# Neighbourhood attention: the layer-norm variance computed in a scores bank, one step later

## The chip, the cores and the metric

The kernel runs on one core of a Trainium2 chip. The metric is the device time of one execution in microseconds; lower is better. Everything is float32 unless a row says bf16.

## The reference, cut to what matters

A tower of token features, neighbourhood attention, a mixture of experts, a decayed attention and soft experts runs over 32 sequences of 512 tokens with 64 features. Between them stand layer norms without weights. The part that the change touches is the attention and the norm behind it:

```
h = h + _L0_attn_ref(_layernorm(h, axis=-1), ...)   # 31 neighbours, dilation 2, 8 heads of 8
h = h + _L0_ffn_ref(_layernorm(h, axis=-1), ...)    # this second norm is prepared inside the attention

def _layernorm(x, axis=-1, eps=1e-05):
    m = jnp.mean(x, axis=axis, keepdims=True)
    v = jnp.var(x, axis=axis, keepdims=True)
    return (x - m) / jnp.sqrt(v + eps)
```

The mean is taken out elsewhere (the features are kept in a basis where it is zero), so a norm is: squares of `h`, their mean over the 64 features (the variance), the logarithm and an exponential (together 1/sqrt), and a product.

## The kernel before, in words

The 32 sequences are 16 pairs (NP = 16); a pair's `h` is one 128 x 512 tile, the two sequences on two halves of the partitions. The attention with dilation 2 splits into even and odd tokens, so `neighbourhood_attention` (from L881) works on 32 units: unit u is pair u // 2 with even (u % 2 = 0) or odd tokens.

Each engine's program is written out by `unrolled` (L577): for step n = -6 ... 31 it calls a list of stages, each with a lead, on unit n + lead. The order of a list is the order in which that engine does the work. On TensorE (PE) a step is: scores of unit n+4 (`scores`, L1040: a mask by 16 bf16 matmuls, L1050, then 32 matmuls, L1056); in an even step the values of n+4 (`window_values`, L1001, matmul L1016), in an odd one the queries of a pair (L991); transposes of half 1 of the exponentials of n+3 (L1065); attention values of half 0 (L1079); keys of a pair (L984, even steps) or odd values (L1016, odd steps); attention values of half 1; transposes of half 0 of unit n+4; in even steps the projection of a pair (`project`, L1038), in odd steps the transposition of a pair's output (`turn`, L1028). Last, in steps 7, 15, 23 and 31, comes `spreads` (L1084): the variance of the quad of pairs that was finished last, four matmuls (L494) that put the means of the squares `s.sq` into 4 x 32 partitions.

PSUM has these tiles here: `p_s`, two tiles of two banks each, the scores of half 0 and half 1; `p_t`, two banks for the transposes; `p_o` for the attention values; and `p_m`, one bank that queries, keys, window values, the turned output, the projection and, before the change, the variance share one after another. Who may write `p_m` next is settled by waits: the variance waits for `s_otd` (ScalarE has copied the turned output out of `p_m`, L1154), and the next even values wait for `s.n_rstd` (ScalarE is done with the variance).

VectorE (DVE) takes for each half of the scores a maximum (L1176) and a difference (L1179, signal `s_diff`, one for each half of each unit), normalises (L1186, L1189), and adds the projection to `h` (L1198, signal `s_h`). ScalarE (ACT) takes the exponentials (L1139), copies transposes (L1146), values (L1133), keys (L1116), queries (L1109) and the turned output (L1154) out of PSUM, and for the norm does `deviations` (L1156): the logarithm (L1161, signal `s.n_ln`) and the exponential (L1163, signal `s.n_rstd`) of the variance. GpSimd (POOL) spreads the keys by head (L917), squares `h` (L487, signal `s.n_sq`) and scales it (L522) when a quad's 1/sqrt has come back. SP sends that result out (`hop`, L500) and back, broadcast over partitions (`spread`, L512), in `n_bc`.

Of the kernel before, what the change touches and what calls it, by code (L numbers as in the profile page):

```python
# [27 lines left out]
ACT = mybir.ActivationFunctionType  # L28
# [3 lines left out]
NP = NB // 2  # L32
NQ = NB // 4
LAST = NP // 4 - 1
# [438 lines left out]
def nth(stage, pair):  # L473

    return NP * stage + pair + 1


def quad(stage, n):

    return NP // 4 * stage + n + 1  # L480
# [47 lines left out]
def done(n):  # L528

    return n + (1 + CREDITS)  # L530
# [350 lines left out]
def neighbourhood_attention(nc, s, v):  # L881

    with ExitStack() as ctx:
# [3 lines left out]
        def ps(name, shape, n=1):  # L887
            return [ctx.enter_context(nc.psum_tensor(f"na_{name}{k}", shape, F32)) for k in range(n)]
# [4 lines left out]
        TURNS = 2 * NP  # L893
# [6 lines left out]
        on = [s.z[:, NP + 8 + k, :].rearrange("p (a b c d) -> p a b c d", a=2, b=2, c=2) for k in range(2)]  # L900
        ot = [s.z[:, NP + 10 + k, :].rearrange("p (two t) -> p two t", two=2) for k in range(2)]
        p_s = ps("ps", [128, 2, HL, 2, WIN], 2)
        p_t, p_o, p_m = ps("pt", [128, GROUPS // 2, 128])[0], ps("po", [128, 512])[0], ps("pm", [128, 512])[0]
        s_q, s_qd, s_k, s_kd, s_blk, s_v, s_vd, s_score, s_max, s_diff, s_e, s_et, s_etd, s_o, s_rden, s_on, s_ot, s_otd, s_out, s_h, s_derived = [
            sem(x) for x in ("q", "qd", "k", "kd", "blk", "v", "vd", "score", "max", "diff", "e", "et", "etd", "o", "rden", "on", "ot", "otd", "out", "h", "derived")]
# [69 lines left out]
        def _(te):  # L975
# [25 lines left out]
            def window_values(at):  # L1001
                j, par = at.of(2), at.k
                te.wait_ge(s_vd, done(at.n - 1))
                if par == 0:
                    te.wait_ge(s_qd, done(j))
                    te.wait_ge(s_otd, done(j - 2))
                    if j >= 6:
                        te.wait_ge(s.n_rstd, quad(1, (j - 6) // 4))
                else:
                    te.wait_ge(s_qd, done(min(j + 1, NP - 1)))  # L1010
                    te.wait_ge(s_h, done(j - 2))
# [28 lines left out]
            def scores(at):  # L1040
                j, par = at.of(2), at.k
                te.wait_ge(s_diff, done(2 * at.n - 1))
                if par == 0:
                    te.wait_ge(s_qd, done(j))
                    te.wait_ge(s_blk, done(j))
# [6 lines left out]
                for half, c, b, f in tiles:  # L1052
                    r = slice(32 * (2 * b + f), 32 * (2 * b + f) + 32)
                    t = 4 * half + c
                    w = window_start(t)
# [13 lines left out]
            def values(b):  # L1069
# [11 lines left out]
                    mm.then_inc(s_o, 1)  # L1081
                return stage

            def spreads(at):  # L1084
                if at.n % 8 == 7:
                    n = at.n // 8
                    te.wait_ge(s.n_sq, nth(1, 4 * n + 3))
                    te.wait_ge(s_otd, done(min(4 * n + 4, NP - 1)))
                    variance(nc, s, n, p_m).then_inc(s.n_var, 1)

            unrolled(TURNS, 2, (4, scores), (4, even_values), (6, queries),
                     (3, transposes(1)), (3, values(0)), (6, keys), (4, odd_values),
                     (3, values(1)), (4, transposes(0)), (1, project), (2, turn), (0, spreads))

        @block.scalar
        def _(sc):
# [52 lines left out]
            def fetch_output(at):  # L1149
                if at.k == 1:  # L1150
# [2 lines left out]
                    sc.wait_ge(s_out, done(j - 2))  # L1153
                    nc.scalar.activation(ot[j % 2].rearrange("p a b -> p (a b)"), p_m[:], ACT.Copy).then_inc(s_otd, 1)  # L1154

            def deviations(at):  # L1156
                if at.n % 8 == 7:
                    n = at.n // 8
                    sc.wait_ge(s.n_var, quad(1, n))
                    sc.wait_ge(s.n_z, nth(0, NP - 1))  # L1160
                    nc.scalar.activation(s.rstd[:, n, :], p_m[:], ACT.Ln, bias=s.eps[:]).then_inc(s.n_ln, 1)  # L1161
                    sc.wait_ge(s.n_ln, 2 + n)
                    nc.scalar.activation(s.rstd[:, n, :], s.rstd[:, n, :], ACT.Exp, scale=-0.5).then_inc(s.n_rstd, 1)  # L1163

            unrolled(TURNS, 2, (4, fetch_even_values), (6, fetch_queries), (3, fetch(1)), (4, exponential(0)),
                     (6, fetch_keys), (4, fetch_odd_values), (4, exponential(1)), (4, fetch(0)), (2, fetch_output), (0, deviations))

        @block.vector
        def _(ve):
# [995 lines left out]
```

## Time and profile before

| | us |
|---|---|
| median of 3 runs | 899.4 |
| lowest, highest | 893.36, 900.43 |
| profiled execution, its own time | 896.55 |
| its span in the trace | 894.8 |
| PE busy | 795.4 (89% of the span) |
| DVE, ACT, POOL busy | 576.0, 476.6, 304.9 |

The attention stage is the stretch from about 98 us to 387 us of the span. PE is the busiest engine there. "PEclk" is the granted clock of TensorE as a share of its full 2.4 GHz; 0.50 is the lower level, 1.2 GHz. In the rows, PEld is the weight load, which overlaps the matmuls, and "idle before" is what the engine stood still ahead of the row, with what ended it.

### The profile page before, as it was taken

To read this page: it belongs to the slowest core of one execution; us is meant where nothing else is said; L and a number is where in the kernel's file an instruction comes from. 1 tells how busy PE (TensorE), PEld (TensorE's weight loads), DVE (VectorE), ACT (ScalarE), POOL (GpSimd) and SP (SyncE) were. 2 spreads that over 40 slices of the span, in tenths; PEclk is the share of its full clock that TensorE was granted. 3 is DMA by queue.
4 is the path that set the end of the run, shared out by engine and by line. 5 is a ranking of instruction groups with operands and counts; after the bars stand their busy time and mean duration, and the time that the engine had idled before them with its cause. 6 is when DMAs were issued, how large, how long until landed. Compare 5 with 4: busy or idle time off the path is not lost. (4 is left out here: it accounts for less than half of the span.)

```text
span 894.8 us, 28767 instructions
## 1 busy us (share of the span) xinstructions
PE 795.4 (89%) x12566; PEld 405.7 (45%) x12566; DVE 576.0 (64%) x849; ACT 476.6 (53%) x656; POOL 304.9 (34%) x296
## 2 busy tenths in 40 slices
PE   4899499999998999758999989799996799999996
PEld 2222177676776766613333223376663233333332
DVE  5537176775775776545877865567673377777776
ACT  2244277776776777536566756422221355555553
POOL 4125553443463352121433455464453620000000
PEclk9889699999999999969999999999998699999998
DMA  4210401001001002010000130053331011111111
GB/s 109 22 28 1 130 28 51 5 4 62 4 4 62 4 5 62 3 60 1 1 2 1 51 92 1 13 167 91 89 94 36 8 30 48 48 49 49 48 49 36
DMA packets 38990, 36.83 MB, mean 41 GB/s; under 512 B 20881, under 2 KB 25138, under 8 KB 38738
## 3 DMA queue, kind: packets, MB, share of 16 engines
q1 hardware_dynamic: 37794, 33.04, 13.2%
q8 instruction: 100, 1.64, 0.8%
q10 hardware_dynamic: 1072, 1.95, 0.7%
q14 instruction: 24, 0.20, 0.1%
HBM read 19.24 MB, written 7.34 MB: 30 GB/s over the span
## 5 line engine op out<-in xcount | busy, mean ns | idle before, releaser
L2043 ACT ACTIVATE se_a<-se_p,cols 128x512 f32<-128x512 f32 x128 | 92.7, 774 | 76.9 <-PE se_p L1996 76.9
L1176 DVE TENSOR_REDUCE na_rowmax<-na_ps 128x16 f32<-128x1024 f32 x64 | 78.0, 1218 | 77.3 <-PE na_ps L1056 77.3
L2063 DVE SCALAR_TENSOR_TENSOR se_a<-se_p,cols,z 128x1024 f32<-128x1024 f32 x64 | 82.2, 1284 | 49.8 <-PE se_p L2006 49.8
L917 POOL TENSOR_TENSOR z<-na_k,const 128x512 f32<-128x512 f32 x64 | 64.6, 1042 | 139.9 <-ACT na_k L1116 139.9
L1418 ACT ACTIVATE z<-me_p,cols 128x512 f32<-128x512 f32 x128 | 81.1, 685 | 55.3 <-PE me_p L1357 50.5
L1550 DVE TENSOR_TENSOR me_gw<-me_pc,z 128x1024 f32<-128x1024 f32 x64 | 78.2, 1222 | 45.2 <-PE me_pc L1369 36.8
L487 POOL TENSOR_TENSOR n_sq<-h 128x512 f32<-128x512 f32 x64 | 68.4, 1074 | 96.2 <-DVE h L839 43.0
L1385 PE MATMUL me_py<-me_gw,w_out 64*64 64x512 f32 x512 | 88.1, 595 | 0.5 <-DVE me_gw L1550 0.5
L1357 PE MATMUL me_p<-z,moe_w 64*64 64x512 f32 x512 | 81.9, 614 | 5.7 <-ACT z L1418 5.7
L522 POOL TENSOR_TENSOR z<-h,n_bc 128x512 f32<-128x512 f32 x60 | 76.3, 1284 | 20.7 <-DMA n_bc<-n_spread 20.7
L1179 DVE TENSOR_TENSOR z<-na_ps,na_rowmax 128x1024 f32<-128x1024 f32 x64 | 78.3, 1224 | 2.2
L1996 PE MATMUL se_p<-z,f_w 64*64 64x512 f32 x512 | 70.5, 618 | 2.7 <-ACTq L535 1.8
L1065 PE MATMUL na_pt<-const,z 128*128 128x128 f32 x512 | 69.9, 280 | 2.6 <-ACT na_et L1146 1.7
L1146 ACT ACTIVATE na_et<-na_pt 128x1024 f32<-128x1024 f32 x64 | 65.4, 1022 | 7.7 <-PE na_pt L1065 6.9
L2006 PE MATMUL se_p<-se_a,f_w 64*64 64x512 f32 x512 | 68.7, 602 | 0.6 <-DVE se_a L2063 0.6
L1139 ACT ACTIVATE z<-z 128x1024 f32<-128x1024 f32 x64 | 67.4, 1053 | 1.7 <-DVE z L1179 0.8
L2018 PE MATMUL se_py<-se_a,w_out 64*64 64x512 f32 x512 | 67.4, 589 | 0.5 <-DVE se_a L2063 0.5
L1065 PEld LDWEIGHTS na_pt<-const,z 128*128 128x128 f32 x512 | 56.7, 142 | 15.6 <-issue 13.3
L1133 ACT ACTIVATE na_v<-na_pm 64x512 f32<-64x512 f32 x64 | 38.6, 602 | 30.2 <-PE na_pm L1016 29.8
L1282 POOL TENSOR_TENSOR h<-h,me_even 128x512 f32<-128x512 f32 x15 | 20.1, 1340 | 99.1 <-DVE me_even L1565 99.1
L1056 PE MATMUL na_ps<-z,na_q 32*32 32x256 f32 x2048 | 52.9, 401 | 0.1
L1079 PEld LDWEIGHTS na_po<-na_v,na_et 128*32 128x32 f32 x4096 | 41.7, 111 | 20.4 <-ACT na_et L1146 11.6
(300 smaller groups left out, 1266.0 us busy)
## 6 DMA issues: line engine op xcount, KB each, us to landing
n_bc<-n_spread SPq DMA_DIRECT2D x120, 128.0 KB, 3.0
z<-z SPq DMA_DIRECT2D x64, 128.0 KB, 2.4
out<-se_rows SPq DMA_DIRECT2D x16, 256.0 KB, 2.1
n_spread<-n_rstd SPq DMA_DIRECT2D x12, 256.0 KB, 2.0
const<-in_const ACTq DMA_DIRECT2D x1, 1050.0 KB, 6.9
const<-in_const ACTq DMA_DIRECT2D x1, 562.0 KB, 4.2
f_w<-in_L_ffn_W SPq DMA_DIRECT2D x4, 128.0 KB
const<-in_const ACTq DMA_DIRECT2D x1, 258.0 KB, 3.0
```

What stands on the lines that cost most here:

```text
L522: return eng.tensor_tensor(row(s.z, p), row(s.h, p), s.bc[p % 4][:], ALU.mult)
L1065: mm = nc.tensor.transpose(p_t[:, c, :], e[b][:, 2 * c:2 * c + 2, :].rearrange("p h w -> p (h w)"), const(s, "ident"))
L1176: nc.vector.tensor_reduce(rowmax[b][:], scored, AX, ALU.max).then_inc(s_max, 1)
L1179: nc.vector.tensor_tensor(e[b], scored, rowmax[b][:].unsqueeze(2).broadcast_to([128, GROUPS, WIN]), ALU.subtract).then_inc(s_diff, 1)
L1357: mm = nc.tensor.matmul(hidden(at.n, b)[half[e2], :], s.moe_w1[half[b], 2 * ep + e2, :], row(s.z, at.of(4))[half[b], :], start=True, stop= ...
L1385: mm = nc.tensor.matmul(p_y[half[b], e2, :], s.moe_w2[half[e2], ep, :], gw[at.k % 2][half[e2], b, :], start=(ep == 0 and b != e2), stop=(e ...
L1418: nc.scalar.activation(g[at.n % 7][:, b, :], hidden(at.n, b)[:], ACT.Gelu, bias=col(s, "moe_b1", ep)).then_inc(s_g, 1)
L1550: nc.vector.tensor_tensor(gw[at.k % 2][:], p_c[:], g[at.n % 7], ALU.mult).then_inc(s_gw, 1)
L1996: mm = nc.tensor.matmul(hidden(at.n, e2)[half[b], :], s.f1_w1[half[e2], 2 * ep + e2, :], z[half[e2], :], start=True, stop=True, skip_group ...
L2006: mm = nc.tensor.matmul(p_2[half[e2], b, :], s.f1_w2[half[b], 2 * ep + e2, :], a1[at.k % 2][half[b], e2, :], start=True, stop=True, skip_g ...
L2043: nc.scalar.activation(a1[at.k % 2][:, e2, :], hidden(at.n, e2)[:], ACT.Relu, scale=col(s, "f1_g1", 2 * ep + e2), bias=col(s, "f1_be1", 2 ...
L2063: nc.vector.scalar_tensor_tensor(out=a2[at.k % 2][:], in0=p_2[:], scalar=col(s, "f1_be2", ep), in1=s.f1_w[:, ep, :].unsqueeze(1).broadcast ...
```

## The change

The variance of quad n is computed one step later (steps 8, 16, 24 instead of 7, 15, 23), in another bank, and at another place within the step: between the attention values of half 1 and the transposes of half 0. The bank is the first of the scores tile of half 0, `p_s[0][:, 0]`. PE waits before it for the squares and for the difference of half 0 of the unit whose scores stand in the bank (unit 8n + 12), and the next unit's scores wait for the logarithm (`s.n_ln`). The even values no longer wait for `s.n_rstd`, the variance no longer waits for `s_otd`. On ACT, logarithm and exponential move with it: from the end of the step to between the exponential of half 1 and the copy of the transposes of half 0. The last quad's variance keeps its place at the very end, behind the loop, in the new bank.

```diff
+        p_var = p_s[0][:, 0].rearrange("p h a w -> p (h a w)")
...
                     te.wait_ge(s_otd, done(j - 2))
-                    if j >= 6:
-                        te.wait_ge(s.n_rstd, quad(1, (j - 6) // 4))
...
                 te.wait_ge(s_diff, done(2 * at.n - 1))
+                if at.n % 8 == 5 and at.n > 8:
+                    te.wait_ge(s.n_ln, 1 + at.n // 8)
...
+            def variance_of(n):
+                te.wait_ge(s.n_sq, nth(1, 4 * n + 3))
+                te.wait_ge(s_diff, done(2 * min(8 * n + 12, TURNS - 1)))
+                variance(nc, s, n, p_var).then_inc(s.n_var, 1)
+
             def spreads(at):
-                if at.n % 8 == 7:
-                    n = at.n // 8
-                    te.wait_ge(s.n_sq, nth(1, 4 * n + 3))
-                    te.wait_ge(s_otd, done(min(4 * n + 4, NP - 1)))
-                    variance(nc, s, n, p_m).then_inc(s.n_var, 1)
+                if at.n % 8 == 0 and at.n > 0:
+                    variance_of(at.n // 8 - 1)
...
-                     (3, values(1)), (4, transposes(0)), (1, project), (2, turn), (0, spreads))
+                     (3, values(1)), (0, spreads), (4, transposes(0)), (1, project), (2, turn))
+            variance_of(LAST)
...
+            def deviations_of(n):
+                sc.wait_ge(s.n_var, quad(1, n))
+                sc.wait_ge(s.n_z, nth(0, NP - 1))
+                nc.scalar.activation(s.rstd[:, n, :], p_var, ACT.Ln, bias=s.eps[:]).then_inc(s.n_ln, 1)
+                sc.wait_ge(s.n_ln, 2 + n)
+                nc.scalar.activation(s.rstd[:, n, :], s.rstd[:, n, :], ACT.Exp, scale=-0.5).then_inc(s.n_rstd, 1)
...
-                     (6, fetch_keys), (4, fetch_odd_values), (4, exponential(1)), (4, fetch(0)), (2, fetch_output), (0, deviations))
+                     (6, fetch_keys), (4, fetch_odd_values), (4, exponential(1)), (0, deviations), (4, fetch(0)), (2, fetch_output))
+            deviations_of(LAST)
```

On PE, around the boundary of steps 7 and 8, the program before reads as follows (`na_pm` is `p_m`, `na_ps` a scores tile, `na_pt` the transposes, `na_po` the attention values; in brackets the semaphores that a row waits for):

```order
295 L1028 MATMUL na_pm<-const,z 128x128 [waits na_h,na_vd,na_on]
296 L1028 MATMUL na_pm<-const,z 128x128 x3
297 L494 MATMUL na_pm<-n_sq,const 32x512 [waits na_otd,n_s_sq]
298 L494 MATMUL na_pm<-n_sq,const 32x512 x3
299 L1050 MATMUL na_ps<-winmask_b,ident_b 32x512 [waits na_blk,na_qd,na_diff]
300 L1050 MATMUL na_ps<-winmask_b,ident_b 32x512 x15
301 L1056 MATMUL na_ps<-z,na_q 32x4x64 x32
302 L1016 MATMUL na_pm<-w_in,z 64x128 [waits na_otd,n_s_rstd,na_qd,na_vd]
```

The same engine in the changed program, from the keys of step 8 to the scores of step 9 (its lines are numbered a little differently: L1080 is the attention values, L1066 the transposes, L1037 the projection, L1051 the mask of the scores):

```order
306 L985 MATMUL na_pm<-z,w_in 128x512 [waits na_otd,na_vd,n_s_z]
307 L1080 MATMUL na_po<-na_v,na_et 32x18 [waits na_on,na_etd]
308 L1080 MATMUL na_po<-na_v,na_et 32x18 x31
309 L494 MATMUL na_ps<-n_sq,const 32x512 [waits na_diff,n_s_sq]
310 L494 MATMUL na_ps<-n_sq,const 32x512 x3
311 L1066 MATMUL na_pt<-const,z 128x128 [waits na_etd,na_e]
312 L1066 MATMUL na_pt<-const,z 128x128 x7
313 L1037 MATMUL na_pm<-z,w_out 128x512 [waits na_vd,na_kd,na_otd]
314 L1051 MATMUL na_ps<-winmask_b,ident_b 32x512 [waits n_s_ln,na_diff]
```

The four variance matmuls have moved from between the turned output and the scores to between attention values and transposes, and the wait for the copied output is gone from them.

On ACT, steps 7 to 9 before (L1139 exponential, L1146 copy of the transposes, L1154 copy of the turned output, L1133 values, L1116 keys, L1109 queries):

```order
116 L1139 ACTIVATE z<-z 128x1024 [waits na_diff]
117 L1146 ACTIVATE na_et<-na_pt 128x1024 [waits na_o,na_et]
118 L1154 ACTIVATE z<-na_pm 128x512 [waits na_out,na_ot]
119 L1161 ACTIVATE n_rstd<-na_pm,eps 128x512 [waits n_s_z,n_s_var]
120 L1163 ACTIVATE n_rstd<-n_rstd 128x512 [waits n_s_ln]
121 L1133 ACTIVATE na_v<-na_pm 64x64x8 [waits na_o,na_v]
```

And ACT in the changed program, in step 8 (L1143 exponential, L1150 copy of the transposes, L1113 queries, L1163 and L1165 logarithm and exponential of the norm):

```order
123 L1120 ACTIVATE na_k<-na_pm,cols 128x512 [waits na_blk,na_k]
124 L1143 ACTIVATE z<-z 128x1024 [waits na_diff]
125 L1163 ACTIVATE n_rstd<-na_ps,eps 128x512 [waits n_s_z,n_s_var]
126 L1165 ACTIVATE n_rstd<-n_rstd 128x512 [waits n_s_ln]
127 L1150 ACTIVATE na_et<-na_pt 128x1024 [waits na_o,na_et]
128 L1113 ACTIVATE na_q<-na_pm,cols 128x512 [waits na_score,na_q]
```

Logarithm and exponential have moved behind the exponential of half 1 of step 8, ahead of the copy of that step's transposes of half 0.

## Rows read from the trace of the kernel before

**Rows 1.** Busy times by stretch (PE, PEld, DVE, ACT, POOL, PEclk, DMA share, GB/s).
```profile
178.00:194.60 16.60, 16.27 (x520) 11.59 (x493) 11.82 (x13) 11.94 (x15) 8.20 (x9) 1.00 0.02 4
194.60:206.60 12.00, 9.97 (x257) 6.36 (x258) 5.49 (x6) 7.64 (x10) 2.60 (x6) 0.86 0.05 18
263.30:275.60 12.30, 10.03 (x256) 6.38 (x258) 5.50 (x7) 7.64 (x10) 4.49 (x5) 0.86 0.02 6
331.80:342.40 10.60, 8.57 (x256) 6.01 (x258) 5.51 (x7) 7.64 (x10) 3.15 (x3) 1.00 0.01 3
```

**Rows 2.** Timeline of DVE: first maximum of units 11, 13, 19, 21, 27, 29.
```profile
194.65 1.22 DVE L1176 TENSOR_REDUCE na_rowmax<-na_ps 128x16 f32<-128x1024 f32 x1 [1.14 <-PE na_ps L1056]
...
214.65 1.22 DVE L1176 TENSOR_REDUCE na_rowmax<-na_ps 128x16 f32<-128x1024 f32 x1 [0.95 <-PE na_ps L1056]
...
263.32 1.22 DVE L1176 TENSOR_REDUCE na_rowmax<-na_ps 128x16 f32<-128x1024 f32 x1 [0.94 <-PE na_ps L1056]
...
283.75 1.23 DVE L1176 TENSOR_REDUCE na_rowmax<-na_ps 128x16 f32<-128x1024 f32 x1 [0.94 <-PE na_ps L1056]
...
331.81 1.23 DVE L1176 TENSOR_REDUCE na_rowmax<-na_ps 128x16 f32<-128x1024 f32 x1 [0.95 <-PE na_ps L1056]
...
350.42 1.23 DVE L1176 TENSOR_REDUCE na_rowmax<-na_ps 128x16 f32<-128x1024 f32 x1 [0.94 <-PE na_ps L1056]
```

**Rows 3.** Timeline of PE, SP and POOL around steps 7 to 9 (first quad).
```profile
202.40 1.44 PE L494 MATMUL na_pm<-n_sq,const 128*32 128x512 f32 x8 [2.03 <-ACT z L1154]
205.26 0.33 SPq L500 DMA_DIRECT2D n_spread<-n_rstd  x1
206.51 1.10 PE L1016 MATMUL na_pm<-w_in,z 128*64 128x128 f32 x16
209.32 5.47 SPq L512 DMA_DIRECT2D n_bc<-n_spread  x8
217.67 1.28 POOL L522 TENSOR_TENSOR z<-h,n_bc 128x512 f32<-128x512 f32 x1
```

**Rows 4.** Timeline of PE, steps 15 and 16 (second quad).
```profile
271.31 1.93 PE L494 MATMUL na_pm<-n_sq,const 128*32 128x512 f32 x8 [2.27 <-ACT z L1154]
275.48 1.10 PE L1016 MATMUL na_pm<-w_in,z 128*64 128x128 f32 x16
```

**Rows 5.** Timeline of PE and ACT, steps 23 and 24 (third quad).
```profile
339.57 1.06 PE L494 MATMUL na_pm<-n_sq,const 128*32 128x512 f32 x8 [2.03 <-ACT z L1154]
340.69 0.69 ACT L1161 ACTIVATE n_rstd<-na_pm,eps 128x512 f32<-128x512 f32 x1 [1.27 <-PE na_pm L494]
341.41 0.63 ACT L1163 ACTIVATE n_rstd<-n_rstd 128x512 f32<-128x512 f32 x1
342.27 1.10 PE L1016 MATMUL na_pm<-w_in,z 128*64 128x128 f32 x16
```

**Rows 6.** Timeline of all engines in steps 10, 11; last row step 12.
```profile
224.00 1.22 DVE L1179 TENSOR_TENSOR z<-na_ps,na_rowmax 128x1024 f32<-128x1024 f32 x1
227.56 1.09 PE L1065 MATMUL na_pt<-const,z 128*128 128x128 f32 x8
227.93 1.06 ACT L1139 ACTIVATE z<-z 128x1024 f32<-128x1024 f32 x1
228.12 4.04 POOL L917 TENSOR_TENSOR z<-na_k,const 128x512 f32<-128x512 f32 x4 [9.17 <-ACT na_k L1116]
228.88 1.02 ACT L1146 ACTIVATE na_et<-na_pt 128x1024 f32<-128x1024 f32 x1
229.44 0.43 PE L1050 MATMUL na_ps<-winmask_b,ident_b 32*32 32x512 bf16 x16
231.68 0.14 PEld L1065 LDWEIGHTS na_pt<-const,z 128*128 128x128 f32 x1 [0.24 <-issue]
239.14 1.10 PE L1016 MATMUL na_pm<-w_in,z 128*64 128x128 f32 x16 [0.44 <-ACT z L1154]
```

**Rows 7.** The page's DMA issues: KB each, median us from issue to landing.
```profile
n_bc<-n_spread SPq DMA_DIRECT2D x120, 128.0 KB, 3.0
```

More of the change, by code:

```diff
@@ L1154, in fetch_output @@
                     nc.scalar.activation(ot[j % 2].rearrange("p a b -> p (a b)"), p_m[:], ACT.Copy).then_inc(s_otd, 1)
-            def deviations(at):
[L1157 to L1163, printed above, removed]
+            def deviations_of(n):
[4 more added lines that the diff above has]
+                nc.scalar.activation(s.rstd[:, n, :], s.rstd[:, n, :], ACT.Exp, scale=-0.5).then_inc(s.n_rstd, 1)
+            def deviations(at):
+                if at.n % 8 == 0 and at.n > 0:
+                    deviations_of(at.n // 8 - 1)
             unrolled(TURNS, 2, (4, fetch_even_values), (6, fetch_queries), (3, fetch(1)), (4, exponential(0)),
-                     (6, fetch_keys), (4, fetch_odd_values), (4, exponential(1)), (4, fetch(0)), (2, fetch_output), (0, deviations))
+                     (6, fetch_keys), (4, fetch_odd_values), (4, exponential(1)), (0, deviations), (4, fetch(0)), (2, fetch_output))
+            deviations_of(LAST)
         @block.vector
```

## The prediction

> **What bounds the kernel now.** I read the page first, for where PE is busy; then the busy times by stretch; then the timeline of DVE, whose first maximum of each unit is a clean beat for the loop; then PE's own timeline at the places where that beat slips. In an undisturbed stretch of the attention (two steps, 16.6 us) PE is busy 16.27 us at full clock, while DVE and ACT stand near 12 us and POOL at 8 [rows 1]. So PE sets the pace there, and a microsecond taken off PE's path in this stage should come off the end. The beat is 16.02 us for two steps: from unit 21 to unit 27 are (331.81 - 283.75) / 3 [rows 2]. Three times the two steps around a variance last longer: 214.65 - 194.65 = 20.00, 283.75 - 263.32 = 20.43, 350.42 - 331.81 = 18.61 [rows 2]. That is 3.98 + 4.41 + 2.59 = 10.98 us over the beat, and this is all that the three variances inside the loop cost today. The fourth stands at the very end of the stage and is outside this count.
>
> **What these 10.98 us are made of.** PE stands still ahead of each variance for 2.03, 2.27 and 2.03 us, and each time what ended the wait is ACT's copy of the turned output [rows 3 to 5]: the variance wants the bank `p_m`, and ACT copies the turned output only behind an exponential and a copy of the transposes. Together 6.33 us. Then the variance itself: 1.06 us at full clock in the third quad [rows 5], 1.44 and 1.93 in the first two [rows 3, 4]. The difference is the clock. The stretches with the first two variances have a mean granted clock of 0.86, the third 1.00 [rows 1]: after its stop PE fell from 2.4 to 1.2 GHz twice and not the third time. From the start of the variance to the even values of the next step it takes 206.51 - 202.40 = 4.11 and 275.48 - 271.31 = 4.17, against 342.27 - 339.57 = 2.70 [rows 3 to 5]. The lower clock costs 1.41 + 1.47 = 2.88 us. The sum of stops, work and clock is 6.33 + 3.18 + 2.88 = 12.39, less what comes back: in an ordinary even step the values wait 0.44 us for the same copy [rows 6], and behind a variance they don't, 3 x 0.44 = 1.32. That gives 11.07 against the measured 10.98, so nothing large is missing.
>
> The Trainium skill says (TensorE: Matmul & The Clock Gate, Part 1: The HAM clock gate) that half clock is the default of an idle TensorE, that sustained work lifts it, and that the penalty is the throttled time times (1 - K/N). The trace agrees that it is the stop that comes first. By the page's formula the first stretch loses 12.0 x 0.14 = 1.68 us where the rows give 1.41; the gain below would be about 0.5 us larger by the page over two quads, and I keep the rows.
>
> **The change part by part.**
>
> 1. The wait of the variance for the turned output goes: -6.33 us. What is late next at the old place? Behind the turned output come the scores, whose waits are met in every ordinary step, and then the even values, which wait 0.44 us for the same copy [rows 6]. So the old cover of the values is gone: +1.32.
>
> 2. The clock is not lost, because with that stop gone PE has no gap in this stretch longer than the 0.44: -2.88 us.
>
> 3. The variance moves between attention values and transposes in the next step. It is the same four matmuls, in a stream that PE bounds, so it is paid in full: 1.06 us each [rows 5]. Before it was paid too, at 1.06 once and more twice, and that surplus stands in term 2. So the new cost is 3 x 1.06 = 3.18 and the old 3.18 cancels. Bounds for one: nothing, if it fell into a stop that the step has anyway, and 1.93 at the lower clock [rows 4]; I take 1.06, since the undisturbed rows leave no stop there.
>
> 4. Its new waits. The squares of the quad are a whole step old. The difference of half 0: in step 10 it runs 224.00 to 225.22, and the place of the variance is 227.56, 2.3 us later [rows 6]. Cost zero, hidden behind values, keys and transposes on PE.
>
> 5. The next scores wait for the logarithm. In step 10's times: ACT ends the exponential of half 1 at 228.99, the variance would end at 227.56 + 1.06 = 228.62, so the logarithm runs 228.99 to 229.68 (0.69, [rows 5]). PE wants its mask at 229.44 + 1.06 = 230.50 [rows 6]. It is met with 0.8 us to spare: zero.
>
> 6. Logarithm and exponential (0.69 + 0.63, and 0.05 between) now stand ahead of the copy of the transposes of half 0 on ACT. That copy ran 228.88 to 229.90 and now ends at about 231.3. Queued behind it on ACT are the copy of the queries and the next copy of transposes. PE needs it for the next transposes, loaded at 231.68 + 1.06 = 232.74 [rows 6]: 1.4 us to spare, zero. If the spare time were gone, each 0.1 us of delay would be 0.1 us of PE, three times.
>
> 7. SP and POOL. The quad's exponential ends at about 230.4 and not before the step. In the first quad SP sent the result off at 205.26 and began to spread it at 209.32, 4.06 us later [rows 3]; 3.0 us more to landing [rows 7]. So the first broadcast lands at about 237.5 in step 10's times. POOL scaled 3.02 us after the maximum of unit 13 (217.67 - 214.65, [rows 2, 3]); in the new program it would stand ready some 2 us before the data come, and wait. Behind that product in POOL's queue come the next pair's keys, which in an ordinary pair start after 9.17 us of idleness [rows 6]. The wait lies in that idleness: zero, with some 7 us to spare.
>
> 8. The last quad: same place at the end, same squares, other bank. Zero.
>
> Sum: -6.33 - 2.88 + 1.32 = -7.89 us; by the beat it is -10.98 + 3.18 = -7.80. I take -7.8. The profiled execution took 896.55, so on its own scale the change gives 888.75. That execution is 2.85 below the median of 899.4, and it was a lucky one in that the third stop did not lower the clock; with a third loss of 1.4 the gain is 9.2. From the median the change then gives 891.6 to 890.2, from the profiled execution 888.75. I say 890.0.
>
> **Rivals.**
>
> A. The clock falls all the same. For it: it fell twice in this stage, and one can't tell from the rows which part of the work around the stop was needed. Against: the stretch with no variance has 1.00 [rows 1]. Then only the stops go: -6.33 + 1.32 = -5.0 us, 893 from the middle of the two scales.
>
> B. ACT becomes the one that is late. The points are those of 5 and 6, whose spare times are 0.8 and 1.4 us and rest on one ordinary step. If ACT's exponential of half 1 comes 1 to 2 us later than in step 10, the scores or the transposes of step 9 stop for about 1 us, three times: -7.8 + 3 = about -5, 893. The Trainium skill says (TensorE: Matmul & The Clock Gate, Part 1: The HAM clock gate, on the queue depths) that ScalarE's queue is strictly first in, first out. By that rule a logarithm that waits for its variance holds the copy behind it too; it changes no price here.
>
> C. Slower. The same mechanism with no cover at all: PE runs variance, then stands until ACT has done logarithm, exponential and the copy of transposes in a row. For one quad that is 1.06 + 0.69 + 0.63 + 1.02 = 3.4 of chain, plus 1.44 for the clock that such a stop costs, 4.84, against 10.98 / 3 = 3.66 now. It is 3 x 1.18 = 3.5 us slower, 900 from the profiled execution and 903 from the median. It decides from a stop of 2.6 us for a quad (3.66 - 1.06). Against it: PE has transposes, projection and scores between the variance and its next need of `p_t`, some 4 us by the rows (227.56 to 231.68, [rows 6]).
>
> D. More than the forecast: the stops lower the clock in all three quads in most executions, and the 0.44 us wait of the values goes as well, since the loop shifts. -7.8 - 1.4 - 1.3 = -10.5, about 887.
>
> E. Nothing: the gain is given back in the next stage. The next stage begins with the last quad's chain, squares, variance, logarithm, which hangs on PE's last projection. It shifts with PE, so I give this little. 898.
>
> **How the numbers follow.** Forecast as worked out 0.64; A 0.08; B 0.11; C 0.05; D 0.09; E 0.03. A measurement of this kernel tells about 1%, 9 us, from no change. The forecast of 7.8 to 9.2 us stands right at that bound, so its 0.64 splits 0.37 above, 0.27 within; D is above; A, B and E are within; of C's 0.05 the price as worked out (0.4%) counts as within, with 0.02, and a longer stop by the same mechanism as slower, with 0.03. That gives faster 0.46, same 0.51, slower 0.03. The range runs from D's 887 less the spread of the runs before (they lie 7 us apart) to A's and B's 893 plus the same on the other side: 884 to 897. C and most of E lie outside.
>
> **What would show it.** Right: in the new profile no stop of PE ahead of the variance, the variance at about 1.06 us at a clock of 1.00 in all three quads, two steps with a variance lasting about 17.1 us by DVE's maxima, the mask of steps 9, 17, 25 not ended by ACT's logarithm, POOL waiting 1 to 5 us for the first broadcast of a quad. Wrong: stops of PE ended by ACT's logarithm or by the copy of the transposes (B, C), a clock below 1.00 in these stretches (A), or a stage that is 8 us shorter while the rest is 8 us longer (E).

## The result, and the profile after

The changed kernel takes 887.67 us (median of 7 runs, 886.72 to 889.2); the kernel before takes 897.07 us (median of 7 runs, 893.36 to 900.43). The ratio is 0.9898 with a 95% interval of 0.9875 to 0.9921: 9.4 us between the medians, 9.2 by the ratio, or 1.0%, faster. The forecast was 890.0 in a range of 884 to 897; it started from a median of 899.4 over three runs. The profiled execution of the changed kernel took 889.17 us, against 896.55 for that of the kernel before: 7.4 us less, where 7.8 were forecast on that scale.

First the page's account of the changed kernel:

```profile
span 887.4 us, 28760 instructions
...
PE 794.3 (90%) x12566; PEld 405.7 (46%) x12566; DVE 577.1 (65%) x849; ACT 475.6 (54%) x656; POOL 304.3 (34%) x296
```

PE did the same number of instructions. Its busy time is 1.1 us lower than before although no work is gone, and the other 6.3 us of the 7.4 by which the span is shorter are time in which PE is not busy. Now the beat, as in [rows 2]: the first maxima of units 11, 12 and 13, of 19, 20 and 21, and of 27, 28 and 29 in DVE's timeline of the changed kernel (start, duration, then what was idle before):

```profile
198.08 1.22 DVE L1183 TENSOR_REDUCE na_rowmax<-na_ps 128x16 f32<-128x1024 f32 x1 [1.12 <-PE na_ps L1057]
205.54 1.23 DVE L1183 TENSOR_REDUCE na_rowmax<-na_ps 128x16 f32<-128x1024 f32 x1 [1.88 <-PE na_ps L1057]
215.19 1.22 DVE L1183 TENSOR_REDUCE na_rowmax<-na_ps 128x16 f32<-128x1024 f32 x1 [0.95 <-PE na_ps L1057]
...
263.26 1.23 DVE L1183 TENSOR_REDUCE na_rowmax<-na_ps 128x16 f32<-128x1024 f32 x1 [0.95 <-PE na_ps L1057]
...
280.11 1.23 DVE L1183 TENSOR_REDUCE na_rowmax<-na_ps 128x16 f32<-128x1024 f32 x1 [0.95 <-PE na_ps L1057]
...
328.04 1.23 DVE L1183 TENSOR_REDUCE na_rowmax<-na_ps 128x16 f32<-128x1024 f32 x1 [0.95 <-PE na_ps L1057]
...
344.87 1.22 DVE L1183 TENSOR_REDUCE na_rowmax<-na_ps 128x16 f32<-128x1024 f32 x1 [0.95 <-PE na_ps L1057]
```

The two steps with a variance take 17.11, 16.85 and 16.83 us where they took 20.00, 20.43 and 18.61. Over three times the beat of 16.02 that is 2.73 us in all instead of 10.98: these three pairs of steps gained 8.25 us. The ordinary pairs became shorter too. Units 13 to 19 and 21 to 27, three pairs each, took 48.67 and 48.06 us before; they take 263.26 - 215.19 = 48.07 and 328.04 - 280.11 = 47.93 now. From the first maximum of unit 11 to that of unit 31 the kernel before takes 171.75 us and the changed one 162.67, so this stretch of the loop gained 9.08 us. Where the 0.83 us beyond the three pairs come from is told below, with the second profiles. The busy times by stretch, one stretch for each in-loop variance, answer to [rows 1] (PE, PEld, DVE, ACT, POOL, PEclk, DMA share, GB/s):

```profile
198.10:215.20 17.10, 16.50 (x499) 11.60 (x500) 11.82 (x14) 13.14 (x17) 6.62 (x11) 1.00 0.05 19
263.30:280.10 16.80, 16.48 (x499) 11.51 (x499) 11.77 (x13) 13.15 (x17) 8.51 (x10) 1.00 0.06 20
328.00:344.90 16.90, 16.57 (x499) 11.58 (x500) 11.85 (x14) 13.14 (x17) 7.26 (x8) 1.00 0.06 19
```

The granted clock is 1.00 in all three; PE is busy 16.5 of 17 us. And step 8 itself, all engines, with the row that answers to [rows 3]:

```profile
210.49 1.07 PE L494 MATMUL na_ps<-n_sq,const 128*32 128x512 f32 x8
...
210.93 1.06 ACT L1143 ACTIVATE z<-z 128x1024 f32<-128x1024 f32 x1
...
211.48 1.09 PE L1066 MATMUL na_pt<-const,z 128*128 128x128 f32 x8
211.88 0.69 ACT L1163 ACTIVATE n_rstd<-na_ps,eps 128x512 f32<-128x512 f32 x1
...
213.13 1.00 ACT L1150 ACTIVATE na_et<-na_pt 128x1024 f32<-128x1024 f32 x1
213.25 0.33 SPq L500 DMA_DIRECT2D n_spread<-n_rstd  x1
213.37 0.43 PE L1051 MATMUL na_ps<-winmask_b,ident_b 32*32 32x512 bf16 x16
...
215.27 1.08 SPq L512 DMA_DIRECT2D n_bc<-n_spread  x2
...
218.89 1.28 POOL L522 TENSOR_TENSOR z<-h,n_bc 128x512 f32<-128x512 f32 x1 [1.61 <-DMA n_bc<-n_spread]
```

The variance has no stop before it; the logarithm ends at 212.57, and the mask that waits for it starts at 213.37 with no stop written beside it. What is new is in the last row: POOL waits 1.61 us for the broadcast (3.27 and 2.70 us in the second and third quad). It costs nothing: POOL then has no work until 228.11.

### The profile page after: what moved, and what is told of

Read it like the earlier page. It is cut to its first block and busy times, and to the rows that moved or that the text cites. A ratio compares the mean times of both kernels' runs of the same rounds, so it can differ in the third digit from the quotient of the medians.

```text
span 887.4 us, 28760 instructions
## 1 busy us (share of the span) xinstructions
PE 794.3 (90%) x12566; PEld 405.7 (46%) x12566; DVE 577.1 (65%) x849; ACT 475.6 (54%) x656; POOL 304.3 (34%) x296
## 3 DMA queue, kind: packets, MB, share of 16 engines
q10 hardware_dynamic: 1072, 1.95, 0.7%
## 5 line engine op out<-in xcount | busy, mean ns | idle before, releaser
L1066 PE MATMUL na_pt<-const,z 128*128 128x128 f32 x512 | 69.8, 280 | 2.5 <-ACT na_et L1150 1.7
L1150 ACT ACTIVATE na_et<-na_pt 128x1024 f32<-128x1024 f32 x64 | 65.4, 1022 | 6.8 <-PE na_pt L1066 6.0
L1143 ACT ACTIVATE z<-z 128x1024 f32<-128x1024 f32 x64 | 67.4, 1053 | 1.6 <-DVE z L1186 1.1
L1066 PEld LDWEIGHTS na_pt<-const,z 128*128 128x128 f32 x512 | 56.9, 142 | 18.2 <-issue 16.2
L1080 PEld LDWEIGHTS na_po<-na_v,na_et 128*32 128x32 f32 x4096 | 41.4, 110 | 20.2 <-ACT na_et L1150 11.9
```

The lines of the kernel that those rows point to most:

```text
L1066: mm = nc.tensor.transpose(p_t[:, c, :], e[b][:, 2 * c:2 * c + 2, :].rearrange("p h w -> p (h w)"), const(s, "ident"))
```

## The experiments

A measure used below: "the three pairs" is the time of units 11 to 13, 19 to 21 and 27 to 29 together, by DVE's first maxima, less three times 16.02. It is 10.98 us for the kernel before and 2.73 for the change. It leaves out the rest of the program, which moves by some microseconds from execution to execution on its own, and it counts only the in-loop part of the change. It also leaves out the ordinary pairs of steps, so where they differ I give the stretch from the first maximum of unit 11 to that of unit 31 beside it: 171.75 us before, 162.67 for the change (171.63 and 162.42 in their second profiles).

### The bank alone

As in the change, the even values' wait for `s.n_rstd` is gone as well.

```diff
-                    te.wait_ge(s_otd, done(min(4 * n + 4, NP - 1)))
-                    variance(nc, s, n, p_m).then_inc(s.n_var, 1)
+                    te.wait_ge(s_diff, done(2 * min(8 * n + 11, TURNS - 1)))
+                    variance(nc, s, n, p_var).then_inc(s.n_var, 1)
...
+                if at.n % 8 == 4 and at.n > 8:
+                    te.wait_ge(s.n_ln, 1 + at.n // 8)
```

> The kernel before with one part of the change: the variance stays at the end of steps 7, 15, 23 (and at ACT's old place), but stands in the scores bank, so it no longer waits for the copied turned output; the next scores wait for the logarithm. Theory of the prediction (what counts is that PE has other work while ACT does its chain): the stop only changes places. PE does the variance at once (1.0 us), then stands ahead of the scores until ACT, behind its copies of transposes and turned output, has done the logarithm: about 1.6 us instead of 2.0 us. Gain 0.4 us of stop and 0.4 us of the values' wait per quad, with the clock as before: 1 to 3 us faster than before, 5 to 7 us slower than the change. Rival (the bank alone is what pays, since p_m was the contended thing): 7 to 8 us faster than before, equal to the change.

Measured: 892.47 us (10 runs), ratio to before 0.9945 (0.9923 to 0.9967); three pairs 6.53 us, that is 4.45 less than before and 3.8 more than the change; units 11 to 31 in 166.24 us. By the medians it is 4.2 us faster than before, where I expected 1 to 3. PE and ACT in its trace, end of step 7:

```profile
200.15 1.07 PE L494 MATMUL na_ps<-n_sq,const 128*32 128x512 f32 x8
200.60 1.02 ACT L1147 ACTIVATE na_et<-na_pt 128x1024 f32<-128x1024 f32 x1
201.52 0.59 ACT L1155 ACTIVATE z<-na_pm 128x512 f32<-128x512 f32 x1
202.00 0.69 ACT L1162 ACTIVATE n_rstd<-na_ps,eps 128x512 f32<-128x512 f32 x1
...
202.79 0.44 PE L1051 MATMUL na_ps<-winmask_b,ident_b 32*32 32x512 bf16 x16 [1.57 <-issue]
```

The stop moved as expected, from ahead of the variance to behind it, 1.57 us instead of 2.03 (the view writes "issue", but the mask follows ACT's logarithm, 202.00 + 0.69, by 0.10). The expectation was off by one thing above all: the clock stayed at 1.00 in all three pairs of this profile, so it gained the clock share too, which I had not counted. The new bank without the new place gains about half of what the change gains, and not all of it: the rival is out.

### The place alone

```diff
-                te.wait_ge(s_diff, done(2 * min(8 * n + 12, TURNS - 1)))
-                variance(nc, s, n, p_var).then_inc(s.n_var, 1)
+                te.wait_ge(s_kd, done(min(4 * n + 7, NP - 1)))
+                te.wait_ge(s_otd, done(min(4 * n + 4, NP - 1)))
+                variance(nc, s, n, p_m).then_inc(s.n_var, 1)
```

(and the projection waits for `s.n_ln` in place of the scores).

> The change with the old bank: the variance stands one step later between attention values and transposes, but in p_m, so it waits for the copy of the keys and the projection waits for the logarithm. Theory: by the rows of step 10 the copied keys are there 0.5 us after PE would want to begin, and the logarithm just before the projection; 0.5 us per quad more than the change, 1.5 us in all: 6 to 7 us faster than before, no stop long enough to lower the clock. Rival (the bank is what pays): the stops come back at 2 us each and the time is within 3 us of before.

Measured: 890.39 us (6 runs), ratio 0.9922 (0.9894 to 0.9949); three pairs 4.73 us, 6.25 less than before, 2.0 more than the change. In its trace:

```profile
208.02 1.06 PE L494 MATMUL na_pm<-n_sq,const 128*32 128x512 f32 x8 [0.51 <-issue]
...
209.14 0.69 ACT L1164 ACTIVATE n_rstd<-na_pm,eps 128x512 f32<-128x512 f32 x1 [0.28 <-PE na_pm L494]
...
209.98 1.10 PE L1039 MATMUL na_pm<-z,w_out 128*128 128x512 f32 x2
```

The 0.5 us that the copied keys come late is there (in all three quads; ACT's copy of the keys ends at 207.92, 0.10 ahead of the variance). So the place alone gains most of it (6.25 of 8.25) even in the contended bank, and once the variance has been moved the bank adds 2.0, of which this stop is 1.5. Units 11 to 31 take 165.63 us, 3.0 more than the change: two ordinary pairs are longer too (16.64 and 16.37 us). In the first of them PE stands 0.53 us inside a row of attention values, where it has nothing to wait for, and the profiles of the put-back stop and of the last version below have the like; its cause is open.

### The clock: the old stop, filled with work

```diff
+                    if n < LAST:
+                        te.wait_ge(s_diff, done(2 * (8 * n + 11)))
+                        for _ in range(2):
+                            variance(nc, s, n, p_var)
                     te.wait_ge(s_otd, done(min(4 * n + 4, NP - 1)))
                     variance(nc, s, n, p_m).then_inc(s.n_var, 1)
```

> The kernel before, with its stop of about 2 us ahead of each in-loop variance filled: the same four variance matmuls are done twice more, into the scores bank, before PE waits for the copied turned output. The length of the stop's place stays about the same; only the clock can change. Theory (the stops lower the clock, 2.88 us of the gain): PEclk 1.00 in the three stretches, variance at 1.06 us each time; 2 to 3.5 us faster than before although work was added. Rival A (the clock falls all the same) and the rival that the clock share was an accident of one execution: same time as before or up to 0.5 us slower.

Measured: 894.91 us (10 runs), ratio 0.998 (0.9964 to 0.9997); three pairs 7.88 us. The program around the boundary of steps 7 and 8, and the stretch from unit 11 to unit 12:

```profile
199.27 1.92 PE L494 MATMUL na_ps<-n_sq,const 128*32 128x512 f32 x16
...
200.64 0.59 ACT L1159 ACTIVATE z<-na_pm 128x512 f32<-128x512 f32 x1
201.29 1.07 PE L494 MATMUL na_pm<-n_sq,const 128*32 128x512 f32 x8
202.28 0.43 PE L1051 MATMUL na_ps<-winmask_b,ident_b 32*32 32x512 bf16 x16
```

```profile
193.62:204.10 10.48, 10.39 (x272) 6.36 (x274) 5.49 (x6) 7.64 (x10) 2.54 (x6) 1.00 0.02 5
```

The row has sixteen more matmuls (eight in the program), and the real variance still starts behind the copied turned output; yet the three pairs are 3.10 us shorter than before, and the clock is 1.00 in all of them. The forecast's clock term was 2.88. Some of it is lost again behind the pairs: units 11 to 31 take 169.38 us, 2.37 less than before. On the whole kernel it is 1.8 us by the medians, with an interval of 0.3 to 3.2 us, a little less than the 2 to 3.5 that I expected. More work where PE would have stood still made the kernel faster, so the clock share is real, and the expectation's rival, no gain at all, is out.

### The stop alone, put back into the change

```diff
+            def stop(at):
+                if at.n % 8 == 7:
+                    te.wait_ge(s_otd, done(min(at.n // 2 + 1, NP - 1)))
...
-                     (3, values(1)), (0, spreads), (4, transposes(0)), (1, project), (2, turn))
+                     (3, values(1)), (0, spreads), (4, transposes(0)), (1, project), (2, turn), (0, stop))
```

> The change with the old stop put back and nothing else: at the end of steps 7, 15 and 23 PE waits for the copied turned output, as the old variance did; the variance stays where the change has it. Theory (stop and clock make the gain): PE stands 2.0 us at each place, the even values' own wait of 0.3 to 0.6 us goes, so 1.6 us per quad, 4.8 us in all; and where the stop lowers the clock another 1.0 to 1.5 us per quad: 4.8 to 9 us slower than the change, 0 to 4 us faster than before. Rival (the gain came from where the variance matmuls stand, not from the stop): within 1 us of the change.

Measured: 894.92 us (10 runs), ratio to before 0.9969 (0.9941 to 0.9996), 7.2 us above the change by the medians. Three pairs 8.77 us, 6.0 more than the change. The middle one is the longest, and it is the one with a lower clock. From the first maxima of units 11 and 19 to the next:

```profile
193.37:202.85 9.48, 7.54 (x248) 5.78 (x250) 5.49 (x6) 6.32 (x8) 2.72 (x6) 1.00 0.01 3
...
260.33:270.37 10.04, 8.10 (x248) 5.95 (x250) 5.49 (x6) 6.32 (x8) 4.47 (x5) 0.93 0.01 3
```

The first and third pair are 18.45 us each, 1.34 and 1.62 over the change, which is the stop of 1.94 us less the values' wait; the second is 19.93, 3.08 over. A wait for one semaphore, with no variance behind it, brings back three quarters of what the change gained. The rival that it was the place of the matmuls is out.

### The price of the variance at its new place

```diff
+                if n < LAST:
+                    variance(nc, s, n, p_var)
                 variance(nc, s, n, p_var).then_inc(s.n_var, 1)
```

> The change with each in-loop variance computed twice in place. Theory (step 3 of the prediction: the variance is paid in full at its new place, PE has no slack there): 0.8 to 1.06 us per quad, 2.5 to 3.2 us slower than the change, the two steps around it 17.9 to 18.1 us. Rival (the 0.83 to 1.1 us that the two steps are over the beat now is a wait of something else, and the matmuls are partly hidden): under 1.5 us slower.

Measured: 892.84 us (10 runs), ratio 0.9957 (0.9935 to 0.998); the pairs take 17.97, 17.80 and 17.70 us, three pairs 5.41, which is 2.68 over the change, or 0.89 for one variance. So the work is paid nearly in full, as step 3 had it, and is not hidden. But the whole kernel is 5 us over the change, and the three pairs explain 2.7 of them. That profile's mixture stage took 173.6 us from the first to the last matmul of its first expert layer, where the change's took 171.6. I ran the same kernel again:

> The kernel with each in-loop variance computed twice, again. Its first profile was 2.7 us longer in the attention loop than the change, but its median 5 us longer, and its mixture stage took 173.6 us against 171.6, with the clock low behind a stop of 2.95 us that the change has too. Theory (the rest is the clock at stops elsewhere, which differs between executions): the mixture stage can come out at 171 or at 174, and the loop's share is 2.7 us again. Rival (the doubled variance causes the rest): 173.6 again and a median near 893.

Measured: 891.61 us (10 runs, 887.36 to 893.63), ratio 0.9947 (0.9922 to 0.9971), three pairs 5.34, mixture stage 173.6 again. The share of the three pairs came back, the median moved by 1.2 us, and the mixture stage did not. Both theories had it half right. The three pairs are not all that the doubled variance costs in the loop: units 11 to 31 take 166.90 and 166.14 us, 3.5 to 4.5 over the change's two profiles. In both executions the pair behind the second variance takes 17.24 and 17.07 us, where the change has 16.09 and 15.91, and PE stands 1.51 and 1.40 us in the middle of eight transposes, up to 284.71 and 283.72. No engine is named as having held it, and its cause is open; that it came back at the same place suggests that it belongs to this program. What is behind the 2 us of the mixture stage can be seen where the traces part, at one stop of PE of 2.95 us, which both kernels have. First the change in its second profile, then the doubled variance in its first:

```profile
510.74 0.41 PE L1376 MATMUL me_pc<-me_ct_parts,pick_b 64*64 64x512 bf16 x4 [2.95 <-DVE me_gw L1557]
510.98 1.03 PE L1392 MATMUL me_py<-me_gw,w_out 64*64 64x512 f32 x8
```

```profile
514.13 0.64 PE L1378 MATMUL me_pc<-me_ct_parts,pick_b 64*64 64x512 bf16 x4 [2.95 <-DVE me_gw L1559]
514.56 1.92 PE L1394 MATMUL me_py<-me_gw,w_out 64*64 64x512 f32 x8
```

The same stop, and behind it the same matmuls at 1.03 and at 1.92 us: the clock once stayed and once fell. All thirteen profiles of this case have the stop, at 2.95 to 2.96 us. Behind it the second row is 1.03 us in seven of them (the first of before, both of the change, the place alone, the filled stop, and the two versions below), with a mixture stage of 171.0 to 172.3 us, and 1.92 us in six (the second of before, the bank alone, the stop alone, ACT's order, both of the doubled variance), with 173.6 to 174.8 us. The kernel before shows both, so it is not tied to a program as such. Whether a kernel can make it likelier, by where it shifts what follows, stays open; one or two profiles of each do not tell.

### ACT's order

```diff
-                     (6, fetch_keys), (4, fetch_odd_values), (4, exponential(1)), (0, deviations), (4, fetch(0)), (2, fetch_output))
+                     (6, fetch_keys), (4, fetch_odd_values), (4, exponential(1)), (4, fetch(0)), (0, deviations), (2, fetch_output))
```

> The change with ACT's logarithm and exponential behind the copy of the transposes of half 0 instead of ahead of it. Theory (steps 5 and 6 of the prediction: the place on ACT matters since the next scores wait for the logarithm, with under 1 us to spare): in the changed trace the transposes end at 212.57, the copy would take 1.0, the logarithm 0.69, so the mask of step 9 starts at about 214.35 instead of 213.37: 1 us per quad, 3 us slower than the change. Rival (the cover is wide enough for either order): same as the change.

Measured: 891.96 us (10 runs), ratio 0.9948 (0.9927 to 0.997); three pairs 5.89 us, 3.16 over the change. In its trace:

```profile
209.42 1.02 ACT L1150 ACTIVATE na_et<-na_pt 128x1024 f32<-128x1024 f32 x1 [0.63 <-PE na_pt L1066]
...
210.34 0.68 ACT L1163 ACTIVATE n_rstd<-na_ps,eps 128x512 f32<-128x512 f32 x1
...
211.16 0.44 PE L1051 MATMUL na_ps<-winmask_b,ident_b 32*32 32x512 bf16 x16 [0.92 <-ACT n_rstd L1163]
```

PE stands 0.92 us for the logarithm. The cover that step 5 counted is as narrow as it said: the same change with two stages of ACT in the other order keeps about half of the gain by the ratios, and 5.1 of 8.25 us in the three pairs.

### The kernel before, and the change, once more

> The change itself once more, for a second profile. Theory: the two steps around each in-loop variance last 16.8 to 17.1 us again with PEclk 1.00, whatever happens elsewhere; first-to-last unit spans may differ by the clock at the stage's start (unit 0 to unit 1 took 7.1 us before and 9.7 us in the changed kernel's first profile). If that start is an accident of the execution, it can come out at either value here; if the change causes it, it is 9.7 again.

> The kernel before once more, for a second profile. The three stops of 2.0, 2.3 and 2.0 us ahead of the variance should be there again. Whether each lowers the clock is what is asked: theory (it depends on how the stop falls, not on the quad): the pattern low, low, full of the first profile need not come back; each quad shows either about 4.0 to 4.4 us over the beat of 16.02 per two steps, or 2.6. Rival (it is fixed by the place in the program): 3.98, 4.41 and 2.59 again.

The change: 887.78 us (4 runs), ratio 0.9899 (0.9868 to 0.9931), three pairs 2.80 us. Its start, unit 0 to unit 1, took 7.09 us, where its first profile had 9.73: that was the clock of one execution (from 108 to 118 us it was 0.50 in the first profile and 0.90 in the second). The kernel before, in one execution of 899.43 us: the three stops are there, 2.04, 2.36 and 2.04 us, and the pairs take 18.61, 20.44 and 20.07. Its stretches from the first maximum of units 11, 19 and 27 to the next:

```profile
194.90:205.50 10.60, 8.56 (x256) 6.01 (x258) 5.50 (x6) 7.64 (x10) 2.75 (x6) 1.00 0.01 3
262.00:274.40 12.40, 10.04 (x258) 6.50 (x260) 5.53 (x7) 7.64 (x10) 4.45 (x5) 0.86 0.04 14
330.50:342.60 12.10, 10.06 (x258) 6.46 (x260) 5.55 (x7) 7.63 (x10) 3.12 (x3) 0.86 0.05 17
```

Full, low, low, where the first profile had low, low, full [rows 1]. The same stop sometimes lowers the clock and sometimes doesn't, and it isn't the quad that decides.

These profiles show one more part of the change, which no step of the prediction priced: the second wait of the even values, for `s.n_rstd`, is gone. The program before has this wait only from unit 12 on (`j >= 6`). Here are the even values of unit 10 and of unit 22 in the first profile of the kernel before, then those of unit 22 in the second profile of the change:

```profile
186.32 1.10 PE L1016 MATMUL na_pm<-w_in,z 128*64 128x128 f32 x16 [0.33 <-ACT z L1154]
...
291.62 1.10 PE L1016 MATMUL na_pm<-w_in,z 128*64 128x128 f32 x16 [0.44 <-ACT z L1154]
```

```profile
285.42 1.10 PE L1015 MATMUL na_pm<-w_in,z 128*64 128x128 f32 x16 [0.33 <-ACT z L1158]
```

Without the wait PE stands 0.33 us, with it 0.44, and the beat follows: in both profiles of the kernel before the pairs from units 3 and 7 take 15.91 to 15.94 us, and those from units 15, 17, 21, 23 and 25 take 16.02 to 16.03. In the change's second profile the same five take 15.91 to 15.93 (in its first, two of them took 16.09). The bank alone, whose ordinary steps differ from the kernel before only by this wait, has 15.91 to 15.94 there, and the filled stop, which kept the wait, has none under 16.03. That is 0.1 us for each ordinary pair; in addition the pair right behind the first variance is 0.4 to 0.55 us shorter, for a reason that I did not trace. Together this makes the 0.8 to 0.95 us that the loop gained beyond the three pairs.

### A bank that fits a stop: two versions

The second stop of a step, 0.3 to 0.6 us ahead of the even values, is left in the change. The attention values' bank `p_o` is free just there.

```diff
-                te.wait_ge(s_diff, done(2 * min(8 * n + 12, TURNS - 1)))
-                variance(nc, s, n, p_var).then_inc(s.n_var, 1)
+                te.wait_ge(s_on, done(min(8 * n + 10, TURNS - 1)))
+                variance(nc, s, n, p_o[:]).then_inc(s.n_var, 1)
...
-            unrolled(TURNS, 2, (4, scores), (4, even_values), (6, queries),
+            unrolled(TURNS, 2, (4, scores), (0, spreads), (4, even_values), (6, queries),
...
+                        if at.n % 8 == 3 and at.n > 8:
+                            te.wait_ge(s.n_ln, 1 + at.n // 8)
```

> A version that may beat both: the variance stands in the bank of the attention values, in steps 8, 16, 24 between scores and even values, where PE waits 0.33 to 0.6 us anyway for the copied turned output; logarithm and exponential stand first on ACT in that step, where ACT is idle for 1.55 us; the attention values of half 0 wait for the logarithm. Theory: the 0.3 to 0.6 us stop hides part of the variance, 1 to 1.5 us faster than the change in all, 885.5 to 887. Rival (ACT's two rows delay the copy of the values and with it keys and attention values): 1 to 3 us slower than the change.

> The version with the variance in the bank of the attention values ahead of the even values, with the exponential of the norm moved away from the logarithm to the end of the step on ACT, so that it no longer delays the copies of the values, which the first version's trace shows starting only behind it (204.00, while PE had the values at 203.70). Theory: 0.3 to 0.6 us less per quad, the two steps at 16.3 to 16.5 us, 1 to 1.5 us faster than the first version and than the change. Rival (values of half 1 are held by something else): within 0.5 us of the first version.

Measured: the first version 888.7 us (8 runs), ratio to before 0.9906 (0.9877 to 0.9935), three pairs 2.35 us; the second, with the exponential moved on ACT, 888.86 us (4 runs), ratio 0.9904 (0.9871 to 0.9937), three pairs 1.92 us. In the three pairs they gain 0.4 and 0.8 us on the change, and on the whole kernel nothing that can be told from no change; units 11 to 31 take 163.07 and 162.15 us, beside 162.67 and 162.42 for the change. I had expected 1 to 1.5 us for either. The second version lies 0.43 us from the first in the three pairs, which is what its rival said. In the second version's trace:

```profile
204.02 1.22 ACT L1137 ACTIVATE na_v<-na_pm 64x512 f32<-64x512 f32 x2 [0.32 <-PE na_pm L1015]
...
206.65 0.33 PEld L1080 LDWEIGHTS na_po<-na_v,na_et 128*32 128x32 f32 x28 [0.76 <-ACT na_et L1150]
```

The copies of the values now start straight behind PE's values (which end at 203.98), so the exponential no longer holds them. I expected 16.3 to 16.5 us for a pair and found 16.96, 16.51 and 16.51. In the second and third of these pairs PE is busy for all of the 16.51 us, so no stop is left to hide work in; the first has a stop of 0.25 us inside its attention values. Neither version beats the change.

## Why the prediction was right

**The bound.** PE set the pace of the stage, and what was taken off its path came off the end: 9.1 us from the loop, 9.4 us by the medians. The two profiled executions are only 7.4 us apart; the one of the change lost 2.6 us to a low clock at the stage's start, which its second profile did not.

**Step 1, the stops (-6.33, and +1.32 back).** Right. No stop stands ahead of the variance in either profile of the change, and the values behind it wait 0.60, 0.32 and 0.33 us, 1.25 in all. Put back alone, a stop of 1.94 us cost 1.34 and 1.62 us per pair where the clock held; the forecast's 2.03 - 0.44 is 1.6. The experiment also shows that a bare wait is enough to bring most of the loss back. The 0.44 us themselves were a reading from behind unit 12 only: 0.11 of them were the price of the second wait, which the change removed and the prediction put at nothing.

**Step 2, the clock (-2.88).** Right. The clock is 1.00 in all three stretches, and filling the old stop with work gained 3.10 us in the three pairs (2.37 over units 11 to 31). The remark that the profiled execution was a lucky one with its third stop was only half right: the second profile of before has a full-clock stop too, another one. Two of three low is what both profiles show. So there is no ground for adding a third 1.4 us. That the medians are 9.4 us apart, close to the 9.2 of that sum, is luck in its composition: in place of a third clock loss there were the dropped second wait with the pair behind the first variance (0.8 to 0.95 us) and a variance cheaper than 1.06. The forecast of 890.0 itself was a middle between two scales; the 7.8 taken from the median of the kernel before as seven runs have it, 897.07, gives 889.3. The stop of the mixture stage, worth some 2 to 3 us between executions, can have moved the medians as well, and no experiment shows that it falls less often in the change.

**Step 3, the variance at its new place (3.18 paid, 3.18 before).** Right in kind, 0.4 us too high: over the beat of 16.02 the pairs cost 1.09, 0.83 and 0.81, together 2.73. Over the change's own beat of 15.92 it is 3.03, of which 0.27 is the longer wait of the first quad's values (0.60 and not 0.33), so that one variance costs 0.92. Doubling it added 0.89 each. The row that follows starts before the variance's row ends (210.49 + 1.07 against 211.48); this overlap I had not credited, and it is 0.08 of the 0.14 to 0.17 us.

**Step 4, the difference.** Right: no wait for it is seen.

**Step 5, the logarithm ahead of the scores, 0.8 us to spare.** Right, to the tenth: 213.37 - 212.57 = 0.80. The experiment on ACT's order used the margin up and stopped PE for 0.92 us.

**Step 6, the copy of the transposes.** Right: it ends at 214.13, 0.76 us after the start of the mask, where 0.8 was forecast, and PE does not stop for it there.

**Step 7, SP and POOL.** Right in kind: POOL waits, 1.61, 3.27 and 2.70 us, at no cost. I had taken 4.06 us between SP's two transfers from one quad; the kernel before has 2.01 and 2.55 in its other two, and the change 2.02, 3.76 and 2.02.

**Step 8.** The last quad kept its chain: the variance waits 1.96 us for the last squares, as before.

**The rivals.** A (the clock falls all the same): refuted by the two traces of the change, with a clock of 1.00 in all six stretches. B (ACT late): did not happen, and the order experiment shows that it would have with two stages swapped, at the price forecast, 3 us. C did not happen; the bank alone comes nearest to its picture (PE standing behind its variance for ACT's chain), and even that was faster than before, since its stop was 1.57 us and not the 2.6 from which C decides. D's figure lies close to the medians, 10.5 against 9.4, but not its mechanism: the clock had fallen at two stops of three in each profile, and of the values' wait 0.11 us went and 0.33 stayed. E: nothing was given back.

## What to carry to other kernels

Ask of a wait on the bounding engine not which semaphore it names but what the engine could do meanwhile: the same matmuls, between two stages that need nothing from them, cost their own time and no more (0.9 us each), while in the old place they dragged a whole chain of another engine in front of them. Moving the work was worth three quarters of the gain here, and the freer bank, on top of it, a quarter; taken in the other order the bank gave half and the place the other half. When such a work is moved, count the margin of every wait that it gets from an ordinary step of the trace; two stages in the wrong order on the helping engine gave about half of it back. And look at waits that are met long before: one such wait, dropped, was worth 0.1 us on PE in each ordinary pair of steps.

And count the clock with the stop: on TensorE a stop of 2 us cost up to 1.5 us more afterwards, at times, so that filling it with useless matmuls paid a little (1.8 us, with an interval of 0.3 to 3.2).

## What was not expected of the hardware

Whether a stop lowers TensorE's clock differs from one execution to the next for the same stop. Of the six stops of 2.03 to 2.36 us in the two profiles of the kernel before, four were followed by 1.2 GHz and two by 2.4 GHz; of the three of 1.94 to 1.95 us in the change with the stop put back, one by the lower; of three of 1.57 us in the bank-alone kernel, none. The stop of 2.95 us in the mixture stage was followed by the lower level in six of thirteen profiles, once with and once without it for the kernel before, and was worth 2 to 3 us.

A wait that was met long before is not free on PE: with the second wait of the even values PE stood 0.44 us, without it 0.33, in the same program and between programs.
